# Sixteen groups of three unread products in the attention schedule of a two-layer tower

## The chip, the core and the metric

The kernel runs on one core of a Trainium2 chip. The metric is the device time of one launch in microseconds, the median of several runs. The engines of the core are TensorE (PE, with its weight loads PEld), VectorE (DVE), ScalarE (ACT), GpSimd (POOL) and SyncE (SP), each with an instruction queue of its own; they meet through semaphores. TensorE writes its results to PSUM, eight banks of 128x512 float32, and VectorE or ScalarE copy them out. TensorE's clock is granted at one of two levels, 1.2 and 2.4 GHz, which the profile shows as 0.50 and 1.00.

## What is computed

```
h = tok(x)                              # relu(x W0) * (x W1), then Wo
h = layernorm(h + attention0(h))        # 16 heads of 16, window |i-j| <= 64
h = layernorm(h + quantised_ffn(h))     # int8-like rows, ternary weights, relu(g)^2 * u
h = layernorm(h + attention1(h))        # 16 heads of 16, causal
h = layernorm(h + moe(h))               # 8 experts, top 2, capacity 640, own layernorm inside
```

There are 4 batches of 512 tokens with 256 channels. Nothing of this is changed by the change: its products are written to PSUM and read by nobody.

## The kernel before

The first part of the kernel (up to about 580 us of the profile) is a software pipeline over 256 attention half steps; the second part is the eight experts and the final norms. A unit `u` is one key tile of four heads of one batch in one layer: 128 units, each of two half steps. At half step `n` the pipeline computes the scores of half `n` (L870), the transposed scores of half `n - 15` (L892), and, every second half step, the products of probabilities and values of half `n - 19` (L908). VectorE takes the row maxima from each score bank (L1159), GpSimd splits them in parts (L576 to L582), ScalarE exponentiates the transposed scores (L683), and GpSimd masks them (`affine_select`, L556, L561, L564). Every eighth half step there is a transpose back of four heads (L918) and a division on VectorE (L1174, L1176).

All else, the dense work, is laid between the half steps by the table `DENSE`: a phase, its index and the half step at which it begins; `STEPS` says how many steps it has. `SCHED` lists for each half step what falls on it. The phases that matter here:

- `o`: output projection and layernorm of one batch in one layer (index 0 to 3 for the first layer). Steps 0 and 1 turn the attention output, steps 2 and 3 multiply (L1031), step 4 takes the moments on VectorE (L1183, L1190, L1194) and the root on GpSimd (L587), steps 5 and 6 write the normed rows on ScalarE (L720).
- `ffn`: the quantised layer. Steps 0 and 1 take row maxima on VectorE (L1276), step 2 scales on ScalarE (L808), step 3 rounds on VectorE (L1294), step 6 transposes (L944 on TensorE, copied by ScalarE at L697), and from step 7 on come the gate and up products (L935).
- `gate` and `route`: logits of the experts (L1068, L1074) and the choice of two of them on VectorE (L1215 to L1270), with the counts on TensorE (L1081, L1084).
- `qkv`: transposes of the normed rows (L925, copied at L702) and the projections (L1005, L1014), with the copies L768 and L769.

The first layer's `o` begins at half steps 54, 86, 118 and 150, its `ffn` at 61, 93, 125 and 157; `route` of batches 0 and 1 begins at 188 and 219.

PSUM banks are given out ahead of time: seven banks rotate (the eighth, `V_BANK`, holds the value sums), and `take` gives each product the bank that came free earliest in the plan. Before TensorE writes a bank it waits until that bank's last content was read (`opened`, `d_open`). On TensorE the order in a half step is: scores, then the early dense work (`early`), then row parts (L877), transposed scores, values, back, and last the other dense work (`dense`).

Once, ahead of the experts, the kernel already has 38 unread products (L1592) of the form that the change uses, `mm(bank(0), identb[:, :], qgu[:, 0, 0:S], start=True, stop=True)`.

Of the kernel before, what the change touches and what calls it, by code (L numbers as in the profile page):

```python
# [147 lines left out]
    return () if t is None else (f"gb{t}", f"ub{t}")  # L148


def stretched(phase, i, c):

    return 2 * c if phase == 'wq' and i or phase == 'send' and i == 1 or phase == 'qkv' and 2 <= i else c
# [27 lines left out]
def dense_take(n, phase, i, key, part):  # L181

    take("d", n, (phase, i, key), READ_LATER.get(phase, {}).get(key[0], 0), part)


for _n in HALVES:
    if 0 <= _n < 2 * UNITS:
        for _i, _ in enumerate(score_heads(_n // 2, _n % 2)):
            take("s", _n, (_n // 2, _n % 2, _i), 0, PARTS[0])
    for _phase, _i, _c in SCHED.get(_n, ()):  # L190
        for _key in early_units(_phase, _c):
            dense_take(_n, _phase, _i, _key, PARTS[4])
    if (_n - TO_ROWS) % 8 == 0 and 0 <= _n - TO_ROWS < 2 * UNITS:
        take("t", _n, ("n", (_n - TO_ROWS) // 8), 0, PARTS[1])
    if 0 <= _n - TO_TURNED < 2 * UNITS:
        _u, _h = divmod(_n - TO_TURNED, 2)
        for _i, _ in enumerate(turned_heads(_u, _h)):
            T_LAST[_u] = (_u, _h, _i)
            take("t", _n, (_u, _h, _i), 0, PARTS[2])
    if (_n - TO_BACK) % 8 == 0 and 0 <= _n - TO_BACK < 2 * UNITS:  # L200
        take("s", _n, ("b", (_n - TO_BACK) // 8), TO_HEADS - TO_BACK, PARTS[3])
    for _phase, _i, _c in SCHED.get(_n, ()):
        for _key in dense_units(_phase, _c):
            dense_take(_n, _phase, _i, _key, PARTS[5])
# [11 lines left out]
def build(nc, xT, w01, wtok, wattn, wo, battn, bvcol, brow, wq0, wdn, wgate, consts, masks, w1, w2, b1, b2, lnrow, out):  # L216
# [3 lines left out]
    with ctx:  # L220
# [122 lines left out]
        with ExitStack() as c2:  # L343
# [498 lines left out]
            def _(pe):  # L842
# [38 lines left out]
                def scores_T(u, half):  # L881
# [6 lines left out]
                    for i, heads in enumerate(turned_heads(u, half)):  # L888
# [4 lines left out]
                                     qs[0:KM, r, hd, lo:hi], start=True, stop=True)  # L893
                        ins.then_inc(t_full((u, half, i))[0], 1)

                def values(u):
                    g, kt = divmod(u, NT)
                    s = u // (NG * NT)
                    lo, hi = q_range(kind_of(u), kt)
                    pe.wait_ge(sel_done, u + 1)  # L900
                    if kt == 0:
                        pe.wait_ge(*d_out(("qkv", s, "v1")))
                    if kt == 0 and g:
                        pe.wait_ge(ot_done, g)
                    p = probs_of(u)
                    for j in range(HG):
                        hd = g % NG * HG + j
                        ins = mm(bank(V_BANK)[32 * j:32 * j + 32, lo:hi],  # L908
                                 vaug[:, s % NV, kt, hd * SLOT:hd * SLOT + 32], p[:, j, :],
                                 start=(kt == 0), stop=(kt == NT - 1), skip_group_check=True,  # L910
                                 tile_position=(0, 32 * j))
                    ins.then_inc(pv_mm, 1)
# [24 lines left out]
                        ins.then_inc(d_full(key)[0], 1)  # L937

                def early(phase, i, c):
                    if phase == "ffn" and c == FQT:  # L940
                        pe.wait_ge(fq_done, i + 1)
                        o = d_open(("ffn", i, "fqT")).bitcast(BF16)
                        for n in range(2 * NT):
                            ins = pe.transpose(o[:, n * P:(n + 1) * P], fqb[:, n * P:(n + 1) * P],  # L944
                                               identb[:, :])
                        ins.then_inc(d_full(("ffn", i, "fqT"))[0], 1)
                    if phase == "ffn" and tile_at(c, 1) is not None:
                        quantised_half(i, tile_at(c, 1), 1)
# [885 lines left out]
```

## Time and profile before

| | before |
|---|---|
| median of 3 runs | 926.13 us (925.48 to 926.74) |
| the profiled execution | 926.73 us |
| its span, first to last instruction | 924.6 us |
| TensorE busy | 834.7 us, 90% |
| VectorE, ScalarE, GpSimd busy | 495.4, 433.1, 376.6 us |
| mean granted TensorE clock | 0.951 |

The profiled execution has 2.1 us around its span and lies 0.6 us above the median. Busy time of TensorE has modelled ends, so it tells where TensorE had anything in flight, not that it worked at its peak. The page also cuts the span in 40 slices with the busy tenths of each engine and the granted clock; the trace gives the same for any stretch.

### The profile page before, as it was taken

How to read it: one execution, taken by the hardware profiler on the slowest of the kernel's cores; microseconds unless marked ns; L12 is line 12 of the kernel's file. 1: busy time of each engine (PE TensorE's matmuls, PEld its weight loads, DVE VectorE, ACT ScalarE, POOL GpSimd, SP SyncE). 2: the span in 40 equal slices, each digit the busy share in tenths (PEclk: the TensorE clock that was granted, in tenths of full speed). 3: DMA queues.
4: the chain of work that ended last, by engine and by line, in shares of the span. 5: the costliest groups of instructions: out<-in, count | busy, mean ns of one | idle time of the engine just before them, and what ended most of it. 6: DMA issues, size and time to landing. Idle time of an engine off the chain costs nothing.

```text
span 924.6 us, 14104 instructions
## 1 busy us (share of the span) xinstructions
PE 834.7 (90%) x4796; PEld 536.8 (58%) x4796; DVE 495.4 (54%) x1899; ACT 433.1 (47%) x792; POOL 376.6 (41%) x549
## 2 busy tenths in 40 slices
PE   6999999899899899899999997699999999999920
PEld 2665546556556455355545454277787787787820
DVE  5675344779788798788768764231131230220246
ACT  1525335688787787888566664132202202112005
POOL 6336224656465373253483635701231221220423
PEclk9999999999899899999899999799999999999975
DMA  9662021212202220210332206420423523512342
GB/s 344 218 232 75 25 70 30 60 53 70 71 7 65 70 55 18 70 47 25 110 99 64 72 31 234 144 75 9 145 50 111 149 27 128 153 19 62 40 108 91
DMA packets 58662, 81.47 MB, mean 88 GB/s; under 512 B 8160, under 2 KB 52193, under 8 KB 56160
## 3 DMA queue, kind: packets, MB, share of 16 engines
q1 hardware_dynamic: 49232, 70.22, 23.6%
q0 software_dynamic: 7296, 9.47, 6.0%
q10 hardware_dynamic: 2064, 0.90, 0.4%
q8 instruction: 38, 0.62, 0.3%
q14 instruction: 32, 0.26, 0.1%
HBM read 35.37 MB, written 19.68 MB: 60 GB/s over the span
## 4 chain that ended last, share of the span: by engine, by line
PE 76%; DVE 11%; issue 4%; ACT 4%; POOL 3%; DMA 1%; SPq 0%; POOLq 0%; ACTq 0%; DVEq 0%
PE ps L1572 15%; PE ps L1586 15%; PE ps L959 6%; PE ps L908 6%; PE ps L1005 5%; PE ps L870 5%; PE ps L892 4%; DVE junk L1159 4%; PE ps L1031 3%; PE ps L976 3%; PE ps L1014 3%; PE ps L925 2%; PE ps L935 2%; ACT probs L683 1%; PE ps L1041 1%
## 5 line engine op out<-in xcount | busy, mean ns | idle before, releaser
L1159 DVE CUSTOM_DVE_ANT_0 junk<-ps,maskb 128x256 bf16<-128x256 f32 (+4 forms) x512 | 200.2, 435 | 82.6 <-PE ps L870 82.1
L683 ACT ACTIVATE probs<-ps 128x512 f32<-128x512 f32 (+1 forms) x304 | 156.9, 551 | 61.0 <-PE ps L892 58.9
L1613 ACT ACTIVATE hTe<-ps,qs 128x640 f32<-128x640 f32 x64 | 50.8, 794 | 218.8 <-PE ps L1572 218.8
L1520 POOL DMA_INDIRECT mixed_rows<-ysb,ids x40 | 62.1, 1553 | 221.4 <-DVE ysb L1688 218.4
L1586 PE MATMUL ps<-ks,hTe 128*128 128x256 f32 x640 | 143.3, 379 | 0.0
L1572 PE MATMUL ps<-dxT,qs 128*128 128x320 f32 x512 | 140.1, 433 | 1.2 <-DVE dxT L1666 1.2
L1586 PEld LDWEIGHTS ps<-ks,hTe 128*128 128x128 f32 x640 | 119.3, 190 | 15.1
L1572 PEld LDWEIGHTS ps<-dxT,qs 128*128 128x128 f32 x512 | 96.7, 190 | 40.5 <-DVE dxT L1666 0.9
L870 PE MATMUL ps<-ks,qs 96*128 96x256 bf16 (+4 forms) x512 | 106.5, 291 | 3.8 <-DVE nmax L1159 2.0
L892 PE MATMUL ps<-qs,ks 99*128 99x256 bf16 (+4 forms) x512 | 103.6, 288 | 6.5 <-DVE nmax L1159 3.5
L908 PE MATMUL ps<-probs,vaug 128*32 128x256 f32 (+4 forms) x1024 | 89.3, 422 | 6.5 <-ACT oT L692 3.3
L870 PEld LDWEIGHTS ps<-ks,qs 96*128 96x128 bf16 x512 | 44.4, 101 | 82.5 <-issue 64.8
L1666 DVE COPY dxT<-ps 128x256 f32<-128x256 f32 x40 | 16.6, 420 | 128.6 <-PE ps L1550 128.6
L561 POOL TENSOR_SCALAR_AFFINE_SELECT probs<-probs 128x256 f32<-128x256 f32 (+1 forms) x64 | 38.4, 600 | 96.1 <-ACT probs L683 95.9
L1685 DVE TENSOR_TENSOR ysb<-ps,ks 128x256 f32<-128x256 f32 x40 | 17.0, 425 | 110.2 <-PE ps L1586 110.2
L556 POOL TENSOR_SCALAR_AFFINE_SELECT probs<-probs 128x512 f32<-128x512 f32 x64 | 41.3, 648 | 66.7 <-ACT probs L683 66.4
L959 PE MATMUL ps<-x_sb,tokw 128*128 128x512 f32 x128 | 61.7, 615 | 7.5 <-DMA tokw<-w 7.5
L892 PEld LDWEIGHTS ps<-qs,ks 99*128 99x128 bf16 x512 | 44.5, 101 | 30.9 <-issue 7.3
L1005 PE MATMUL ps<-actT,aw 128*128 128x512 f32 x128 | 60.5, 598 | 1.9 <-issue 1.1
L1159 DVE DVE_READ_ACCUMULATOR2_ANT nmax<- 128x1 f32 x512 | 42.2, 82 | 0.0
L908 PEld LDWEIGHTS ps<-probs,vaug 128*32 128x32 f32 x1024 | 20.7, 110 | 37.0 <-issue 25.3
L959 PEld LDWEIGHTS ps<-x_sb,tokw 128*128 128x128 f32 x128 | 23.2, 195 | 31.2 <-issue 31.0
(199 smaller groups left out, 1244.3 us busy)
## 6 DMA issues: line engine op xcount, KB each, us to landing
qs<-parts SPq DMA_DIRECT2D x96, 128.0 KB, 2.4
ks<-parts SPq DMA_DIRECT2D x96, 128.0 KB, 2.4
qs<-w SPq DMA_DIRECT2D x8, 1024.0 KB, 9.6
ks<-w SPq DMA_DIRECT2D x8, 1024.0 KB, 4.9
dispatched_rows<-att SPq DMA_DIRECT2D x8, 650.0 KB, 10.9
ks<-dispatched_rows SPq DMA_DIRECT2D x4, 650.0 KB, 7.4
x_sb<-xT SPq DMA_DIRECT2D x8, 256.0 KB, 4.0
mixed_rows<-h SPq DMA_DIRECT2D x4, 512.0 KB, 3.1
```

The lines of the kernel that those rows point to most:

```text
L556: pool.affine_select(out=p[:, :, 0:P], in_=p[:, :, 0:P], compare_op=ALU.is_ge, fill=0.0, base=0, pattern=[[0, HG], [1, P]], channel_multip ...
L683: act.activation(probs_of(u)[:, heads[0]:heads[-1] + 1, :], turned_bank((u, half, i))[:, 0:len(heads) * w].rearrange("p (j n) -> p j n", n=w),
L870: ins = mm(o[:, a * (hi - lo):(a + 1) * (hi - lo)], qs[0:KS, r, hd, t * P:(t + 1) * P], ks[0:KS, r, hd, lo:hi], start=True, stop=True)
L892: ins = mm(o[:, a * (hi - lo):(a + 1) * (hi - lo)], ks[0:KM, r, hd, kt * P:(kt + 1) * P], qs[0:KM, r, hd, lo:hi], start=True, stop=True)
L908: ins = mm(bank(V_BANK)[32 * j:32 * j + 32, lo:hi], vaug[:, s % NV, kt, hd * SLOT:hd * SLOT + 32], p[:, j, :], start=(kt == 0), stop=(kt = ...
L959: ins = mm(o, tokw[:, k, col:col + P], x_sb[:, k, :], start=(k == 0), stop=(k == KD - 1))
L1005: ins = mm(o, w[:, k, col:col + P], actT[:, k, :], start=(k == 0), stop=(k == KD - 1))
L1159: ins = dve.tensor_tensor_reduce(out=junk[:, b - (b > V_BANK), a * (hi - lo):(a + 1) * (hi - lo)], in0=score_bank((u, half, i))[:, a * (hi ...
L1520: pool.indirect_dma_start(out=acc, out_offset=bass.IndirectOffsetOnAxis(ap=ids[:, e, t:t + 1], axis=0), in_=ysb[:, e % 2, t, :], in_offset ...
L1572: ins = mm(bank(2 * (n % 2) + c)[:, 0:HC], w1s[:, e % 2, k, m * P:(m + 1) * P], dxT[:, e % 2, k, c * HC:(c + 1) * HC], start=(k == 0), sto ...
L1586: ins = mm(bank(4 + n % 2)[:, 0:D], hTe[:, e % 2, m, t * P:(t + 1) * P], w2s[:, e % 2, m, :], start=(m == 0), stop=(m == MH - 1))
L1613: act.activation(hTe[:, e % 2, m, :].rearrange("p (a n) -> p a n", a=2), ps[:, 2 * (n % 2):2 * (n % 2) + 2, 0:HC], ACT.Silu, bias=b1s[:, e ...
```

## The change

Three unread products, 128x512 in bfloat16 each, are put at certain half steps as early work, right behind the scores of that half step and ahead of the transposed scores. They take a bank of the rotation, wait until its former content was read, write it three times, and count it as filled and as read themselves. The condition `filled_up` holds for steps 4 and 6 of `o` of the first layer's four batches (half steps 58 and 60, 90 and 92, 122 and 124, 154 and 156), for step 0 of the four `ffn` (61, 93, 125, 157), and for steps 2 and 3 of `route` of batches 0 and 1 (190, 191, 221, 222): 16 half steps and 48 products. The plan of banks is made anew with these takes in it; 82 of the other takes have another use before them than they had, all of them within eight half steps behind a group.

```
+UNREAD = 3
+
+def filled_up(phase, i, c):
+    return (phase == "o" and i < B and c in (4, 6) or phase == "ffn" and c == 0
+            or phase == "route" and i < 2 and c in (2, 3))
...
     for _phase, _i, _c in SCHED.get(_n, ()):
+        if filled_up(_phase, _i, _c):
+            dense_take(_n, _phase, _i, f"x{_c}", PARTS[4])
         for _key in early_units(_phase, _c):
...
+                def unread(key, count):
+                    o = d_open(key)
+                    for n in range(count):
+                        ins = mm(o, identb[:, :], qgu[:, 0, 0:S], start=True, stop=True)
+                        if n == 0:
+                            ins.then_inc(d_full(key)[0], 1)
+                    ins.then_inc(d_out(key)[0], 1)
...
                 def early(phase, i, c):
+                    if filled_up(phase, i, c):
+                        if phase == "o" and i == 0 and c == 4:
+                            pe.wait_ge(w_taken, 2)
+                        unread((phase, i, f"x{c}"), UNREAD)
```

On TensorE, at half steps 58 to 61, the program before reads as follows (L870 scores, L892 transposed scores, L908 values, L918 back):

```order
L870 MATMUL ps<-ks,qs 128x256 x2
L892 MATMUL ps<-qs,ks 128x256 x2
L870 MATMUL ps<-ks,qs 128x256 x2
L877 MATMUL ps<-identb,nparts 48x128
L892 MATMUL ps<-qs,ks 128x256 x2
L908 MATMUL ps<-probs,vaug 32x192 x4
L870 MATMUL ps<-ks,qs 128x256 x2
L892 MATMUL ps<-qs,ks 128x256 x2
L918 MATMUL ps<-cst,oT 128x128 x4
L870 MATMUL ps<-ks,qs 128x256 x2
L892 MATMUL ps<-qs,ks 128x192 x2
```

And after the change, with the same work under new line numbers (L881 scores, L903 transposed scores, L928 values, L938 back, L911 the unread products):

```order
L881 MATMUL ps<-ks,qs 128x256 x2
L911 MATMUL ps<-qgu,identb 128x512 x3
L903 MATMUL ps<-qs,ks 128x256 x2
L881 MATMUL ps<-ks,qs 128x256 x2
L888 MATMUL ps<-identb,nparts 48x128
L903 MATMUL ps<-qs,ks 128x256 x2
L928 MATMUL ps<-probs,vaug 32x192 x4
L881 MATMUL ps<-ks,qs 128x256 x2
L911 MATMUL ps<-qgu,identb 128x512 x3
L903 MATMUL ps<-qs,ks 128x256 x2
L938 MATMUL ps<-cst,oT 128x128 x4
L881 MATMUL ps<-ks,qs 128x256 x2
```

Nothing else moved: a group of three now stands between the scores and the transposed scores at half steps 58 and 60, and a third one follows the last row shown, at 61. The second place is the routing of batch 0 on TensorE, at half steps 190 to 192; after the change it reads:

```order
L881 MATMUL ps<-ks,qs 128x512 x2
L911 MATMUL ps<-qgu,identb 128x512 x3
L881 MATMUL ps<-ks,qs 128x512 x2
L911 MATMUL ps<-qgu,identb 128x512 x3
L903 MATMUL ps<-qs,ks 128x512 x2
L928 MATMUL ps<-probs,vaug 32x256 x4
```

and before:

```order
L870 MATMUL ps<-ks,qs 128x512 x4
L892 MATMUL ps<-qs,ks 128x512 x2
L908 MATMUL ps<-probs,vaug 32x256 x4
L870 MATMUL ps<-ks,qs 128x128 x2
L892 MATMUL ps<-qs,ks 128x512 x2
```

Here the second pair of scores has three unread products ahead of it and the transposed scores have six.

## Rows read from the trace of the kernel before

**Rows 1.** The page: span, and TensorE's granted clock in 40 slices, in tenths.
```profile
span 924.6 us, 14104 instructions
...
PEclk9999999999899899999899999799999999999975
```
**Rows 2.** Busy time by stretch: us from:to, length, PE PEld DVE ACT POOL, clock, DMA.
```profile
178.30:181.70 3.40, 1.88 (x20) 0.84 (x18) 3.37 (x17) 1.97 (x5) 1.57 (x3) 0.99 0.02 5
181.70:188.50 6.80, 5.92 (x37) 3.73 (x37) 5.03 (x26) 6.32 (x14) 4.68 (x12) 0.50 0.60 162
...
243.10:249.90 6.80, 5.94 (x37) 3.82 (x38) 4.97 (x26) 6.23 (x14) 4.68 (x12) 0.50 0.75 203
...
304.60:311.40 6.80, 6.06 (x39) 3.86 (x40) 4.57 (x26) 6.24 (x14) 4.89 (x12) 0.50 0.74 203
...
376.20:379.60 3.40, 3.33 (x18) 2.69 (x18) 1.72 (x10) 3.40 (x9) 1.64 (x3) 0.50 0.56 153
...
441.10:447.90 6.80, 6.80 (x30) 3.47 (x31) 5.30 (x24) 2.33 (x5) 1.77 (x4) 0.50 0.20 54
...
505.90:512.70 6.80, 6.69 (x32) 2.01 (x32) 4.48 (x28) 4.10 (x9) 2.07 (x6) 0.50 0.60 179
```
**Rows 3.** Timeline of PE from half step 61 on: start, us, what, idle before.
```profile
178.03 0.38 PE L870 MATMUL ps<-ks,qs 96*128 96x256 bf16 x2
179.09 0.34 PE L892 MATMUL ps<-qs,ks 99*128 99x192 bf16 x2 [0.68 <-DVE nmax L1159]
...
181.45 0.33 PE L892 MATMUL ps<-qs,ks 99*128 99x192 bf16 x2 [0.84 <-ACT probs L683]
182.66 1.08 PE L908 MATMUL ps<-probs,vaug 128*32 128x256 f32 x8 [0.88 <-POOL probs L564]
...
186.80 1.87 PE L925 MATMUL ps<-cst,h 128*128 128x128 f32 x8
...
191.11 1.03 PE L935 MATMUL ps<-qgu,work 128*128 128x512 bf16 x4
```
**Rows 4.** Busy time by stretch, columns as in Rows 2.
```profile
182.20:190.70 8.50, 8.04 (x62) 5.18 (x63) 5.37 (x27) 7.59 (x17) 4.61 (x11) 0.63 0.63 170
...
373.70:381.30 7.60, 6.54 (x45) 3.81 (x45) 4.35 (x22) 7.16 (x16) 2.62 (x6) 0.78 0.44 120
364.70:371.50 6.80, 6.46 (x46) 2.62 (x44) 6.52 (x29) 4.21 (x11) 2.49 (x4) 1.00 0.14 36
...
446.20:451.00 4.80, 4.22 (x31) 1.51 (x27) 4.52 (x22) 2.27 (x6) 0.87 (x5) 0.82 0.74 200
498.80:506.40 7.60, 6.00 (x45) 2.34 (x43) 7.19 (x28) 4.10 (x10) 1.73 (x4) 0.97 0.50 135
...
178.00:182.70 4.70, 2.29 (x26) 1.01 (x27) 4.50 (x24) 2.97 (x7) 2.47 (x4) 0.89 0.18 45
...
221.40:224.90 3.50, 2.17 (x24) 1.01 (x22) 3.36 (x10) 3.44 (x7) 2.49 (x5) 1.00 0.50 141
```
**Rows 5.** Timeline of POOL and ACT around the same place.
```profile
177.32 0.64 POOL L564 TENSOR_SCALAR_AFFINE_SELECT probs<-probs 128x512 f32<-128x512 f32 x1
...
178.37 1.04 POOL L587 TENSOR_TENSOR rstd<-mv,neg_half 128x4 f32<-128x4 f32 x1 [0.41 <-DVE mv L1194]
...
189.71 1.00 ACT L697 ACTIVATE work<-ps 128x1024 bf16<-128x1024 bf16 x1
```
**Rows 6.** The chain that ended last, in time, at 176 to 196: start, us, what.
```profile
178.37 1.05 POOL rstd L587
...
182.66 1.08 PE ps L908 x8
...
187.00 1.66 PE ps L925 x8
```
**Rows 7.** Timeline of DVE and ACT at 371 us and in the routing, where they meet PE.
```profile
371.33 0.68 DVE L1159 CUSTOM_DVE_ANT_0 junk<-ps,maskb 128x512 bf16<-128x512 f32 x1
...
448.38 1.09 ACT L683 ACTIVATE probs<-ps 128x512 f32<-128x512 f32 x2 [2.84 <-PE ps L892]
...
451.13 0.87 ACT L683 ACTIVATE probs<-ps 128x384 f32<-128x384 f32 x2 [0.47 <-PE ps L892]
...
512.74 0.56 DVE L1159 CUSTOM_DVE_ANT_0 junk<-ps,maskb 128x384 bf16<-128x384 f32 x1 [2.15 <-PE ps L870]
```

## The prediction

> **What bounds the kernel now.** I read the clock row of the page first. TensorE is granted full speed nearly everywhere, with an 8 in slices 11, 14, 17 and 23 and a 7 in slice 26 [rows 1]. Then I cut the places of the dips out as stretches [rows 2]. There are six ahead of 520 us: 1.2 GHz for 6.8 us from 181.7, from 243.1, from 304.6, from 441.1 and from 505.9, and for 3.4 us from 376.2. The first four belong to `o` and the start of `ffn` of batches 0 to 3, the last two to `route` of batches 0 and 1. That is where the change puts its products, so its effect must be read there.
>
> What comes before such a fall is to be seen at the first one, which the second and third repeat nearly to the tenth. From 178.3 to 181.7 TensorE was busy 1.88 of 3.40 us and VectorE 3.37 [rows 2]. TensorE waits three times, 0.68 us for row maxima, 0.84 us for ScalarE, 0.88 us for GpSimd's mask [rows 3]. So ahead of the fall the chain runs over VectorE, the root on GpSimd at 178.37, and ScalarE [rows 6], and TensorE has 4.70 - 2.29 = 2.41 us to spare between 178.0 and 182.7 [rows 4]. From 182.66 on the chain lies on TensorE [rows 6], now at half clock. So the spare time is where products cost little, and the stretch behind it is where the clock is worth something.
>
> **What the change adds.** Per group three products of the form of L935, of which four take 1.03 us with the end of the last modelled at 0.38 us: (1.03 - 0.38) / 3 = 0.217 us each [rows 3]. A group is 0.65 us at full clock and twice that, 1.3 us, at half. 48 of them are 10.4 us of TensorE. The waits for banks cost nothing where I followed them: the bank of a group was last used two half steps earlier or more, and VectorE or ScalarE has read it by then. The one wait for the quantised weights is long fulfilled.
>
> **Batches 0 to 2 (three times the same).** The three groups are 1.95 us against 2.41 us of spare time, so they nearly fit. One thing leaks: the group at half step 58 stands ahead of the transposed scores, so ScalarE's exponentials and GpSimd's masks of that step come 0.65 us later. The second mask ends at 177.32 + 0.64 = 177.96 and the root starts at 178.37 [rows 5], so 0.41 us of the 0.65 are covered and the root, on the chain, is late by 0.24 us. The rest of the groups pushes scores and values into what was idle; VectorE has its scores in time.
>
> Does the clock then stay? The spare time in 178.0 to 182.7 sinks from 2.41 to some 0.7 us (2.41 - 1.95 + 0.24), a busy share of 85%. The trace has a stretch without a fall that is much thinner than that: 221.4 to 224.9, TensorE busy 2.17 of 3.50 us, 62%, clock 1.00 [rows 4]. Nearest to it on the other side is 178.3 to 181.7 with 55%. So I take the clock as kept.
>
> What a kept clock brings is not half of 6.8 us. On the chain TensorE has 188.5 - 182.66 = 5.8 us at half clock, so the upper bound is 2.9 us. But ScalarE is next: from 182.2 to 190.7, where its copy L697 of the first quantised transposes ends (189.71 + 1.00 [rows 5]), it is busy 7.59 of 8.50 us [rows 4]. It can only lose its 0.91 us of idle time. TensorE's gate product L935 needs that copy and starts today at 191.11 [rows 3], 0.40 us after it, because TensorE itself was late; at full clock that goes too. 0.91 + 0.40 = 1.3 us, less the 0.24 of the late root: 1.0 us gained per batch, with 0 and 2.9 us as bounds. I take the value of the ScalarE row, since it is measured at the place. Three times: **-3.0 us**. From 191 on TensorE bounds, and keeps the gain.
>
> **Batch 3.** Here the causal units begin and TensorE has hardly any room: 6.80 - 6.46 = 0.34 us from 364.7 to 371.5 [rows 4]. 1.95 - 0.34 = 1.6 us of products push the scores back. VectorE, which carries the chain there, takes the maxima of half step 158 at 371.33 [rows 7], about 0.9 us after TensorE had them, so it is late by 0.6 to 0.7 us. The late scores close the later gap, so the fall at 376.2 should go as well. It covers 3.4 us, so at most 1.7 us come back; ScalarE has only 0.44 us of idle time from 373.7 to 381.3 [rows 4], with a wait like the one at L935 behind it. I take 1.0 us back and 0.6 us lost: **-0.4 us** (bounds +1.6 and -1.7).
>
> **Routing of batch 0.** The fall at 441.1 comes before the groups of half steps 190 and 191, which lie at 446.2 and later; nothing of the change is ahead of it, so it stays. The first group runs at half clock, 1.3 us, the second at full, 0.65 us, together 1.9 us, against 0.58 us of TensorE's idle time from 446.2 to 451.0 [rows 4]. So the transposed scores come some 1.3 us later. ScalarE waits for them today (2.84 us), and has 0.47 us to spare before its next wait [rows 7]; VectorE, on the chain, has its scores early enough. Bounds 0 and +1.9 us; I take **+0.5 us**, near ScalarE's slack.
>
> **Routing of batch 1.** VectorE is busy 7.19 of 7.60 us from 498.8 to 506.4, TensorE idle 1.6 us [rows 4], so two groups (1.3 us) are hidden. They are over by 503.3, and TensorE stays thin after that, up to the fall at 505.9. I take this fall as staying: **0**. If it went, the stretch after it is TensorE's alone, with VectorE waiting 2.15 us at its end [rows 7]: -2.5 us.
>
> **Sum.** -3.0 - 0.4 + 0.5 + 0 = -2.9 us. Against the profiled execution, 926.73 us (span 924.6), that is 923.8 us; that execution lies 0.6 us above the median, so against 926.13 us it is **923.2 us**.
>
> **A rule that speaks against it.** TensorE ran from 186.80 to 188.67 nothing but the transposes of L925 [rows 3], and the clock rose at 188.5 [rows 2]. The Trainium skill, TensorE: Matmul & The Clock Gate, Part 4: PE-mode transpose, says that the full clock doesn't engage for transposes, because they don't count as busy in the same way. The trace does not agree, since the clock rose at the end of just such a stretch. What the rule's result would be here: the fall is only put off to the transposes that stand in each of the four batches, nothing comes back, and 3 x 0.24 + 0.6 + 0.5 = +1.8 us are lost. I give that 0.03 and count it with rival 2.
>
> **Rivals.**
> 1. *The fall in the routing of batch 1 goes too.* For it: the groups end 2.6 us ahead of it. Against: TensorE stays thin to the last. -2.9 - 2.5 = -5.4: 920.7 us.
> 2. *Slower: falls are moved into TensorE's own stretches.* If the clock is lost some 3.4 us later, at about 185, again for 6.8 us, it stays low until 191.9, where TensorE is the chain. The 3.4 us from 188.5 to 191.9 then run at half speed, 1.7 us more, while 185 to 188.5 is half clock in both. At full clock from 181.7 to 185 TensorE wins at most 1.2 us, since ScalarE bounds. So +0.5, with the late root +0.7 per batch: +2.1, for batch 3 +0.6, routing +0.5: +3.2 us, 929.3 us. It decides from the moment that the clock is not granted at 185. Against it: the 85% above.
> 3. *The gain is taken back.* All that follows moves against the moments at which the clock is decided. The stretch at 221.4 and one like it at 283 are thin; a fall in one puts 6.8 us of half clock where TensorE bounds for much of it, some 2 to 3 us. -2.9 + 2.5 = -0.4: 925.7 us. Or the falls stay and the products are hidden but for the late roots and the routing: +0.7 + 0.5 = +1.2: 927.3 us. Between them 926.5 us.
>
> **Chances.** Forecast 0.48, rival 1 0.14, rival 2 0.14, rival 3 0.24. A measurement tells about 0.2%, 1.9 us, from no change. Forecast and rival 1 are faster by more, but for some 0.06 of the forecast where the gain per batch is nearer 0.6 us: faster 0.56. Rival 3 and that: same 0.30. Rival 2: slower 0.14. The range reaches from rival 1 with a little more from ScalarE's side (920.0) to short of rival 2 (927.8).
>
> **What would show it.** Right: the stretches after half steps 58, 90 and 122 at clock 1.00, ScalarE without idle time up to L697, the interval from one `o` to the next shorter by 1.0 us, the fall by the logits of batch 0 still there. Batch 3: the maxima of half step 158 0.6 us later against the work before. Wrong: a clock of 0.50 within 8 us behind any first-layer group, or a new one near 221 or 283 us; GpSimd's root later by more than 0.24 us; or TensorE late at half step 62, which would say that the groups did not fit in the waits.

## The result, and the profile after

| | before | changed |
|---|---|---|
| median beside each other on one chip | 925.95 us (925.48 to 926.74, 4 runs) | 919.64 us (919.21 to 921.91, 4 runs) |
| ratio, 95% interval | | 0.9934 (0.9919 to 0.9949) |
| profiled execution, span | 926.73, 924.6 us | 921.91, 919.8 us |
| mean granted TensorE clock | 0.951 | 0.963 |

The changed kernel is faster by 6.3 us. Forecast were 2.9 us: the sign was right, the time lies below the low end of the range (920.0). Run again on two chips ("all, again" and "all, third" below) it stood at 0.9937 (0.9920 to 0.9953) and 0.9943 (0.9921 to 0.9964), by the medians 5.9 and 5.8 us. The profiled execution of the changed kernel is the slowest of its four. On the chip of the first four experiments two of the 26 runs of before took 1,592 and 1,707 us; they are left out of its median below.

The page of the changed kernel: span, busy time (14,178 instructions are 74 more than before: 48 weight loads and 25 of the 48 products, of which some have no record in the trace) and the clock row.

```profile
span 919.8 us, 14178 instructions
...
PE 833.0 (91%) x4821; PEld 535.8 (58%) x4844; DVE 497.2 (54%) x1899; ACT 430.7 (47%) x792; POOL 376.2 (41%) x549
...
PEclk9999999999999999999899998799999999999975
```

Ahead of 620 us the row of before [rows 1] has an 8 in slices 11, 14 and 20 and a 7 in slice 26. Now 11 and 14 show a 9, 20 still an 8 and 26 a 7, and slice 25 has a new 8: the fall at 567.4 us of before stands at 552.1, and the long one behind it begins at 572.6. There are 48 products more, and yet TensorE is busy 1.7 us less.

The places of the falls, cut out as in [rows 2] and [rows 4]: us from:to, length, PE PEld DVE ACT POOL, clock, DMA.

```profile
176.90:180.30 3.40, 3.40 (x28) 1.83 (x27) 3.33 (x18) 1.35 (x3) 1.94 (x3) 1.00 0.04 8
183.10:190.60 7.50, 6.10 (x65) 3.87 (x65) 6.04 (x33) 7.46 (x17) 4.90 (x12) 1.00 0.67 182
224.40:227.90 3.50, 3.26 (x16) 2.59 (x17) 2.69 (x14) 2.54 (x5) 0.56 (x1) 0.51 0.02 4
285.90:289.30 3.40, 3.40 (x18) 2.60 (x17) 2.78 (x13) 2.24 (x3) 0.39 (x2) 0.50 0.02 4
372.80:376.20 3.40, 2.30 (x18) 0.69 (x16) 3.01 (x15) 3.05 (x7) 1.34 (x4) 1.00 0.74 200
439.50:446.30 6.80, 6.58 (x30) 3.41 (x31) 5.51 (x24) 2.23 (x5) 1.76 (x4) 0.50 0.23 61
504.80:511.40 6.60, 6.38 (x55) 2.90 (x55) 6.36 (x37) 4.71 (x11) 3.29 (x8) 1.00 0.67 198
```

The falls behind the groups of batches 0 to 3 are gone, and so is the one in the routing of batch 1. The one in the routing of batch 0 stays. Two new ones of 3.4 us have come, at 224.4 and 285.9.

A half step is one turn of the pipeline, and a stage is here the time from one half step to another. To see what each fall is worth I read the start of the scores (L870 before, L881 after) of certain half steps from the timeline of PE, in every profiled execution, and took the differences. A stage is named by its half steps. For the first stage the two starts are, before, 168.30 and 195.60, and here in the changed kernel:

```profile
169.17 0.34 PE L881 MATMUL ps<-ks,qs 96*128 96x192 bf16 x2
...
195.14 0.34 PE L881 MATMUL ps<-ks,qs 96*128 96x192 bf16 x2
```

27.3 us became 26.0. All stages, in us ("all, again" and "all, third" are the changed kernel run again; the others are the experiments below; the last column is the span). Left out are 134 to 150 (36.2 or 36.3 everywhere), 167 to 186 (46.2 everywhere), 199 to 217 (32.4 to 32.9) and 232 to 255 (30.0 or 30.4).

| profiled execution | 54-70 | 70-86 | 86-102 | 102-118 | 118-134 | 150-167 | 186-199 | 217-232 | span |
|---|---|---|---|---|---|---|---|---|---|
| before | 27.3 | 32.3 | 29.1 | 32.3 | 29.5 | 34.6 | 24.2 | 24.3 | 924.6 |
| changed | 26.0 | 33.9 | 27.2 | 34.0 | 27.8 | 33.8 | 24.6 | 21.7 | 919.8 |
| all, again | 26.0 | 32.3 | 27.7 | 34.0 | 27.8 | 33.8 | 24.6 | 21.7 | 917.3 |
| all, third | 26.0 | 32.3 | 27.7 | 34.0 | 27.8 | 33.8 | 23.9 | 21.5 | 918.6 |
| first layer | 26.0 | 32.3 | 27.7 | 33.9 | 27.8 | 33.8 | 24.5 | 21.7 | 921.2 |
| routing only | 26.1 | 32.3 | 27.9 | 32.3 | 29.5 | 34.6 | 24.6 | 21.7 | 922.9 |
| eight columns | 27.4 | 32.3 | 29.1 | 32.3 | 29.6 | 34.7 | 24.1 | 21.7 | 921.9 |
| no routing 0 | 26.0 | 33.9 | 27.3 | 34.0 | 27.8 | 33.8 | 24.1 | 21.7 | 920.1 |
| guarded | 26.0 | 32.3 | 27.6 | 32.3 | 28.2 | 33.8 | 26.1 | 21.7 | 919.1 |
| no batch 3 | 26.0 | 32.3 | 27.7 | 34.0 | 27.8 | 34.3 | 23.8 | 21.7 | 916.2 |
| one group | 25.6 | 32.3 | 27.3 | 32.3 | 27.9 | 33.3 | 23.8 | 21.7 | 914.1 |
| one group, again | 25.6 | 32.3 | 27.3 | 32.3 | 27.9 | 34.3 | 26.3 | 21.7 | 921.6 |
| one group, routing 0 | 25.6 | 32.3 | 27.3 | 32.3 | 27.9 | 33.3 | 23.8 | 24.3 | 917.6 |
| one group, routing 1 | 25.6 | 32.3 | 27.3 | 32.3 | 27.9 | 33.3 | 26.2 | 21.7 | 918.1 |
| one group alone | 25.6 | 32.3 | 27.3 | 32.3 | 27.9 | 34.3 | 26.1 | 21.7 | 921.5 |
| early group | 26.4 | 32.3 | 28.2 | 33.9 | 28.2 | 34.3 | 26.2 | 24.6 | 927.8 |
| one product | 26.1 | 33.9 | 27.4 | 34.0 | 27.4 | 34.4 | 26.5 | 24.6 | 926.6 |
| late start | 27.7 | 32.3 | 29.2 | 32.3 | 29.6 | 34.7 | 24.1 | 21.7 | 930.0 |

The sum for "all, again" against before, up to the scores of half step 255 (541.0 against 546.8), in unrounded starts: -0.4 at the start, -1.3 and -1.4 and -1.8 for batches 0 to 2, +1.7 for the new fall at 284, -0.8 for batch 3, +0.4 and -2.7 for the two routings, and +0.4 for 232 to 255: -5.8 us. The last +0.4 belongs to the routing of batch 1: that stage takes 30.0 us in the four profiles with its fall and 30.4 in the fourteen without, so the missing fall is worth 2.3 us, not 2.7. Behind half step 255, where nothing was changed, "all, again" takes 376.3 us against 377.8, another -1.5; but "all, third", the same kernel, takes 378.1 there.

The first three falls can be counted over all eighteen profiles. In the twelve with a group of three full products at step 0 of `ffn` none of the three is there. In the six without it ("before", "routing only", "eight columns", "early group", "one product", "late start") the first and second are always there, with 3.4 or 6.8 us, and the third is missing in "one product" alone.

### The profile page after: what moved, and what is told of

It reads as the page before. It is cut to its first block, busy times and chain, and to the rows that moved or that the text cites. A ratio compares the mean times of both kernels' runs of the same rounds, so it can differ in the third digit from the quotient of the medians.

```text
span 919.8 us, 14178 instructions
## 1 busy us (share of the span) xinstructions
PE 833.0 (91%) x4821; PEld 535.8 (58%) x4844; DVE 497.2 (54%) x1899; ACT 430.7 (47%) x792; POOL 376.2 (41%) x549
## 4 chain that ended last, share of the span: by engine, by line
PE 74%; DVE 8%; ACT 5%; issue 5%; POOL 4%; DMA 3%; SPq 0%; POOLq 0%; ACTq 0%; DVEq 0%
PE ps L1596 15%; PE ps L1610 15%; PE ps L983 6%; PE ps L928 5%; PE ps L1029 5%; PE ps L881 5%; PE ps L903 4%; PE ps L1000 3%; PE ps L1055 3%; PE ps L1038 3%; DVE junk L1183 3%; PE ps L955 2%; ACT probs L694 2%; POOL dispatched_rows L632 2%; PE ps L1065 2%
## 5 line engine op out<-in xcount | busy, mean ns | idle before, releaser
L1637 ACT ACTIVATE hTe<-ps,qs 128x640 f32<-128x640 f32 x64 | 50.8, 794 | 218.4 <-PE ps L1596 218.4
L881 PE MATMUL ps<-ks,qs 96*128 96x256 bf16 (+4 forms) x512 | 104.1, 285 | 2.5 <-DVE nmax L1183 1.3
L903 PE MATMUL ps<-qs,ks 99*128 99x256 bf16 (+4 forms) x512 | 101.2, 284 | 1.4 <-DVE nmax L1183 0.9
L928 PE MATMUL ps<-probs,vaug 128*32 128x256 f32 (+4 forms) x1024 | 86.6, 410 | 6.4 <-ACT oT L703 3.2
L881 PEld LDWEIGHTS ps<-ks,qs 96*128 96x128 bf16 x512 | 43.2, 99 | 79.0 <-issue 61.4
L1029 PE MATMUL ps<-actT,aw 128*128 128x512 f32 x128 | 60.5, 598 | 1.9 <-issue 1.1
L903 PEld LDWEIGHTS ps<-qs,ks 99*128 99x128 bf16 x512 | 43.9, 99 | 25.6 <-issue 3.1
L928 PEld LDWEIGHTS ps<-probs,vaug 128*32 128x32 f32 x1024 | 20.4, 108 | 36.6 <-issue 23.6
```

Source lines behind the costliest of these rows:

```text
L881: ins = mm(o[:, a * (hi - lo):(a + 1) * (hi - lo)], qs[0:KS, r, hd, t * P:(t + 1) * P], ks[0:KS, r, hd, lo:hi], start=True, stop=True)
L903: ins = mm(o[:, a * (hi - lo):(a + 1) * (hi - lo)], ks[0:KM, r, hd, kt * P:(kt + 1) * P], qs[0:KM, r, hd, lo:hi], start=True, stop=True)
L928: ins = mm(bank(V_BANK)[32 * j:32 * j + 32, lo:hi], vaug[:, s % NV, kt, hd * SLOT:hd * SLOT + 32], p[:, j, :], start=(kt == 0), stop=(kt = ...
L1029: ins = mm(o, w[:, k, col:col + P], actT[:, k, :], start=(k == 0), stop=(k == KD - 1))
L1637: act.activation(hTe[:, e % 2, m, :].rearrange("p (a n) -> p a n", a=2), ps[:, 2 * (n % 2):2 * (n % 2) + 2, 0:HC], ACT.Silu, bias=b1s[:, e ...
```

## The experiments

**First layer alone** (the groups of `route` left out) and **routing alone** (those of `o` and `ffn` left out). Here and below, where the group of step 4 of `o` of batch 0 is left out and others stay, the one wait for the quantised weights moves to the first group that is left; "early group" keeps it.

```
 def filled_up(phase, i, c):
-    return (phase == "o" and i < B and c in (4, 6) or phase == "ffn" and c == 0
-            or phase == "route" and i < 2 and c in (2, 3))
+    return phase == "o" and i < B and c in (4, 6) or phase == "ffn" and c == 0
```
```
+    return phase == "route" and i < 2 and c in (2, 3)
```

> Only the twelve groups of the first layer's o and ffn; the four of the routing are left out. Theory A (each group works where it stands: a kept clock brings 1.4 us per batch 0 to 2, 0.8 us for batch 3, and the two groups of routing 1 alone keep the clock there): the fall near 500 to 510 us comes back, the time is 2.0 to 2.5 us above the changed kernel, about 921.8 us. Rival B (the fall in routing 1 went only because everything before it had moved by some us): no fall there either, and about 919.2 us.

> Only the four groups of the two routings; the twelve of the first layer are left out, so all falls up to 441 us stay where they were. Theory A: the fall at 505.9 is gone, -2.5 us there, +0.4 us for routing 0: about 923.9 us. Rival B: the fall at 505.9 stays, about 926.4 us.

Measured: the first layer alone 923.98 us, ratio 0.9975 (0.9960 to 0.9990); routing alone 927.49 us, 1.0005 (0.9993 to 1.0016), where before took 926.96 us on that chip. The table shows the first layer's gain without the routing's groups: 26.0, 27.7, 27.8 and 33.8. The two medians together give 2.4 us less than before, not the 6: in single executions more than the edit differs. In "first layer" the fall in the routing of batch 1 is missing although no group is there (21.7), and the time behind half step 255 is 379.5 us, 1.4 to 3.2 us more than in the three profiles of the changed kernel; in "routing only" the falls at 183 and 244 last 3.4 us, not 6.8, although nothing stands ahead of them that before doesn't have, and stages 54 to 70 and 86 to 102 are 1.2 us shorter (26.1, 27.9). So a profile of one execution can't price a group, and a stage is only as good as the number of executions that agree.

**Eight columns.** Each product is cut to 8 of its 512 columns; banks, waits and places are as in the changed kernel. It asks whether the gain is the clock's or that of the new plan of banks.

```
-                        ins = mm(o, identb[:, :], qgu[:, 0, 0:S], start=True, stop=True)
+                        ins = mm(o[:, 0:8], identb[:, :], qgu[:, 0, 0:8], start=True, stop=True)
```

> All sixteen groups, the same plan of banks and the same waits, but each unread product has 8 columns instead of 512, so there is next to no work in them. Theory A (the gain is the clock's): all six falls stay, time 926 us, within 0.5 us. Rival C (the gain comes from the other plan of banks): 920 to 922 us.

Measured: 925.13 us, 0.9987 (0.9975 to 1.0000). The falls of batches 0 to 2 are where they were, 6.8 us each, and the stages are before's to 0.1 us: 27.4, 29.1, 29.6, 34.7. The line of the products in the groups of this kernel, and under it the stretch of the first fall:

```profile
L911 PE MATMUL ps<-qgu,identb 128*128 128x8 bf16 x48 | 3.6, 169 | 0.7 <-DVE att L1200 0.7
```
```profile
182.10:188.90 6.80, 6.10 (x38) 3.92 (x39) 4.78 (x24) 6.08 (x14) 4.68 (x12) 0.50 0.74 200
```

So in the first layer the gain is the clock's: it needs the columns, not the banks. In the routing of batch 1 this kernel has no fall either (21.7), which is taken up below.

**No routing 0** (the groups of batch 0's routing left out) and **no batch 3** (those of `o` and `ffn` of batch 3 left out).

```
-            or phase == "route" and i < 2 and c in (2, 3))
+            or phase == "route" and i == 1 and c in (2, 3))
```
```
-    return (phase == "o" and i < B and c in (4, 6) or phase == "ffn" and c == 0
+    return (phase == "o" and i < 3 and c in (4, 6) or phase == "ffn" and i < 3 and c == 0
```

> The changed kernel without the two groups of routing 0 (half steps 190 and 191). Theory A: they lie behind a fall that has already happened and cost 0.4 us, so 919.2 us. Rival D: they help the clock to rise sooner or keep it later, so 920 us or more.

> Without the three groups of batch 3 (half steps 154, 156, 157). Theory A2: the fall near 376 us is back and the groups' cost of 0.6 us gone; half steps 150 to 167 took 34.6 us before and 33.8 with the groups, so the time is 0.8 us above the changed kernel. Rival: the fall at that place hangs on the moment only, and leaving the groups out changes nothing or gains 0.6 us.

Measured: 922.44 us, 0.9961 (0.9944 to 0.9979) without routing 0, the chip of the first three; 919.88 us, 0.9935 (0.9918 to 0.9952) without batch 3, beside 920.15 for the changed kernel on its chip. In the stages: with the groups in routing 0 it takes 24.6 us, without them 24.1, since the fall stays at 439.7; that is the 0.5 us of the forecast. Batch 3 takes 33.8 us with its groups, 34.6 in before and 34.3 here, where the fall (372.2) is still 3.4 us long. So they bring 0.5 to 0.8 us in the stage, which the medians can't confirm: without them the kernel is 0.3 us faster, within the noise.

**Guarded** (no groups in routing 0, and one more group at step 22 of `ffn` of batches 0 and 1, half steps 83 and 115, ahead of the new falls).

```
-    return (phase == "o" and i < B and c in (4, 6) or phase == "ffn" and c == 0
-            or phase == "route" and i < 2 and c in (2, 3))
+    return (phase == "o" and i < B and c in (4, 6) or phase == "ffn" and (c == 0 or i < 2 and c == 22)
+            or phase == "route" and i == 1 and c in (2, 3))
```

> The changed kernel once more, as the yardstick for the others of this call and for a second look at its falls. Theory A2 (what the first four runs left: the groups of the first layer keep the clock where they stand; the thin stretches near 221, 283 and 506 us and in 548 to 553 fall or not by where they lie against the moments at which the clock is decided): the stretches from half step 54 to 70 and from 118 to 134 take 25.9 and 27.8 us again, those near 221 and 283 may fall or not, and with it the time moves by 1.6 us each. Rival: the falls at 221 and 283 are there every time.

> Without the two groups of routing 0, and with one more group at half steps 83 and 115 (step 22 of ffn of batches 0 and 1), where TensorE waits 0.75 and 0.78 us for ScalarE. Theory A2: no fall near 221 and 283, half steps 70 to 86 and 102 to 118 take 32.3 us as before the change instead of 33.9; with routing 0 at -0.5 us that is 1 to 3.5 us below the changed kernel of this call, the more the oftener those falls come. Rival: the added 1.3 us of products are on the chain, and the time is the same or longer.

Measured: guarded 920.24 us, 0.9930 (0.9911 to 0.9949); the changed kernel again 920.15 us, 0.9937. In the guarded kernel both thin stretches are at full clock, 32.3 and 32.3 us. The changed kernel has a fall at 283.5 in this profile too, but none at 224. The same stretches, "all, again" and then "guarded":

```profile
219.00:227.00 8.00, 6.46 (x74) 4.24 (x73) 7.72 (x32) 7.23 (x14) 4.24 (x7) 1.00 0.31 84
283.50:286.90 3.40, 3.40 (x17) 2.67 (x18) 2.64 (x13) 2.33 (x4) 0.29 (x2) 0.50 0.02 4
```
```profile
219.00:227.00 8.00, 7.11 (x65) 4.18 (x64) 7.72 (x31) 7.55 (x14) 4.81 (x7) 1.00 0.44 119
```

At 219 the extra group takes TensorE from 6.46 to 7.11 us busy and moves neither VectorE (7.72) nor the stage. That the guards kept the falls away isn't shown by this one profile: "all, again" has none at 221 without a guard, and "one group" below none at 283. What was saved at 283 was lost elsewhere: the routing of batch 0 took 26.1 us, because its fall came later (446.7) and hit TensorE's own stretch.

**One group.** Only the group at step 0 of each first-layer `ffn`, the last of the three, right ahead of the thin stretch; with the routing's groups (twice, on two chips), alone, and with one routing each.

```
-    return (phase == "o" and i < B and c in (4, 6) or phase == "ffn" and c == 0
+    return (phase == "ffn" and c == 0
             or phase == "route" and i < 2 and c in (2, 3))
```

> Of the three groups per batch in the first layer only the one at step 0 of ffn (half steps 61, 93, 125, 157); the routing groups as in the change. Theory E (what counts is that the stretch just ahead of the fall holds products; the earlier groups only make GpSimd's root 0.3 us late): the clock is kept, half steps 54 to 70 take 25.6 us, and the time is about 1 us below the changed kernel. Theory F (all three are needed, since they push TensorE's own work into the gap): the falls are back, 27.3 us for 54 to 70, and the time is 3 to 5 us above the changed kernel.

> Only the one group per batch at step 0 of ffn (half steps 61, 93, 125, 157), no groups in the routing: 12 products in all. Theory A2 (the routing groups buy nothing that lasts; the stretch 217 to 232 takes 21.7 us without them too): the same as with the routing groups, 915.5 to 917.5 us. Rival: the groups of routing 0 or 1 do keep the clock in the routings, and without them 2 to 3 us are lost: 918 to 919 us.

> The one-group kernel with both routings' groups once more, on the chip of this call. Theory K (the groups of routing 0 keep the clock whenever the fall would come late, at 445 us and after, and cost 0.5 us when it comes early): 915.5 to 918 us, half steps 186 to 199 in 23.8 or 24.6 us, never 26.1. Rival L (916 us was that chip's luck): 920 to 923 us, as the kernel without routing groups took on another chip.

> One group per batch in the first layer and the groups of routing 0 only. Theory K: half steps 186 to 199 in 23.8 or 24.6 us; the time within 1 us of the kernel with both routings' groups. Rival L: 26.1 us for 186 to 199, 920 to 923 us.

> One group per batch in the first layer and the groups of routing 1 only. Theory K: half steps 186 to 199 in 24.1 or 26.1 us, and the time 1 to 4 us above the kernel with both routings' groups. Rival L: no difference between the two.

> The changed kernel, for the same chip. Theory K: 919 to 921 us, 186 to 199 in 24.6 or 23.8 us; 2 to 5 us above the one-group kernel, of which 0.9 to 1.2 us from GpSimd's root in four batches and the rest from falls near 221 and 283 us that the one-group kernel misses. Rival L: the two within 1 us.

| | us | ratio to before, 95% |
|---|---|---|
| one group | 915.92 | 0.9901 (0.9876 to 0.9925) |
| all, again (same chip) | 920.15 | 0.9937 (0.9920 to 0.9953) |
| one group alone | 921.98 | 0.9948 (0.9928 to 0.9968) |
| one group, again | 923.26 | 0.9947 (0.9927 to 0.9966) |
| one group, routing 0 | 920.88 | 0.9938 (0.9914 to 0.9961) |
| one group, routing 1 | 921.29 | 0.9938 (0.9917 to 0.9960) |
| all, third (same chip as the last three) | 921.66 | 0.9943 (0.9921 to 0.9964) |

In all five the first three falls are gone with a third of the products, the first stage takes 25.6 us (26.0 with three groups), and no new fall comes at 224 or 283. The 0.4 us (25.6 in place of 26.0) go with the root, since here nothing stands ahead of the transposed scores of half step 58. It starts 10.1 us behind half step 54, as before; in the changed kernel 10.4 us. "One group", then the changed kernel, timeline of POOL:

```profile
178.48 1.04 POOL L598 TENSOR_TENSOR rstd<-mv,neg_half 128x4 f32<-128x4 f32 x1 [0.41 <-DVE mv L1218]
```
```profile
179.58 1.04 POOL L598 TENSOR_TENSOR rstd<-mv,neg_half 128x4 f32<-128x4 f32 x1
```

The group itself lies in a wait, which the timeline of PE of "one group" shows, and the values behind it follow after a wait for GpSimd's mask as before:

```profile
179.50 0.59 PE L911 MATMUL ps<-qgu,identb 128*128 128x512 bf16 x2 [0.99 <-DVE nmax L1183]
...
182.76 0.64 PE L928 MATMUL ps<-probs,vaug 128*32 128x256 f32 x8 [0.79 <-POOL probs L575]
```

But its total isn't settled: the same kernel took 915.9 us on one chip and 923.3 on another, 4.2 us under the changed kernel there and 1.6 us over it here. Five of the six runs on the first chip took 915.5 to 916.5 us and one 921.8; the seven on the other took 920.6 to 923.7. The two profiles differ mainly in three places: 150 to 167 (33.3 and 34.3), 186 to 199 (23.8 and 26.3), and the time behind half step 255 (376.2 and 379.8). In each the second has a fall that the first hasn't. Behind 255 that explains a part only: from the first to the last product of the experts the fall at 595 makes 286.1 us of 284.9, 1.2 us more, but 2.5 us lie ahead of it, up to the first of these products (50.8 and 53.3), where both have a fall of 13.7 us. "One group", then the three of "one group, again":

```profile
PEclk9999999999999999999999999799999999999975
```
```profile
370.00:373.40 3.40, 3.38 (x19) 1.99 (x20) 2.41 (x14) 3.40 (x9) 1.98 (x5) 0.50 0.54 144
445.10:451.90 6.80, 6.80 (x38) 2.33 (x38) 4.46 (x25) 3.45 (x8) 1.90 (x6) 0.50 0.44 135
595.30:598.70 3.40, 2.88 (x9) 1.60 (x8) 0.91 (x3) 0.00 (x0) 3.40 (x6) 0.50 0.13 44
```

The fall in routing 0 was absent in "one group", "no batch 3" and "one group, routing 0", early (437 to 442) or short in most others, and late (444 to 450) in six (that of "late start", at 445.3, counts as early by its own start); late the stage takes 26.1 to 26.5 us, against 24.1 or 24.2 for an early one of 6.8 us (24.6 with the groups in place) and 23.8 for none. With two full groups there it came late in 1 of 8 profiled executions, without them in 5 of 10. Theory K of the expectations is out: with the groups of routing 0 the fall still came late once (26.3 us), and the kernel without them ("routing 1") took 2.0 us less than that one, not 1 to 4 more. In routing 1 the count is clearer: with groups no fall in 10 of 10, without them (or with eight columns) a fall in 4 of 8: before, "one group, routing 0", "early group" and "one product". The nearest pair is "one group, routing 0" and "one group", alike in every stage before, 24.3 and 21.7 us. The fall in the former:

```profile
498.70:505.50 6.80, 6.75 (x32) 2.04 (x33) 4.52 (x28) 4.14 (x9) 2.06 (x6) 0.50 0.61 180
```

**Early group and one product.** Does a smaller edit keep the clock? Tried are the group at step 4 of `o` alone, or the `ffn` group with one product of 512 columns and one of 8; neither has groups in the routings.

```
-    return (phase == "o" and i < B and c in (4, 6) or phase == "ffn" and c == 0
-            or phase == "route" and i < 2 and c in (2, 3))
+    return phase == "o" and i < B and c == 4
```
```
-UNREAD = 3
+UNREAD = 2
...
+    return phase == "ffn" and c == 0
...
-                        ins = mm(o, identb[:, :], qgu[:, 0, 0:S], start=True, stop=True)
+                        cols = 8 if n else S
+                        ins = mm(o[:, 0:cols], identb[:, :], qgu[:, 0, 0:cols], start=True, stop=True)
```

> Only the group at step 4 of o (half steps 58, 90, 122, 154), some 2.5 us earlier than the group of the one-group kernel, no others. Theory E (the products must stand in the thin stretch just ahead of the fall): the falls stay, half steps 54 to 70 take 27.3 us or, with GpSimd's root late, 27.6, and the time is 925 to 927 us. Rival G (any extra products in the neighbourhood do): 54 to 70 in 25.9 us and 919 us or less.

> The one group at step 0 of ffn, but with one product of 512 columns and one of 8 in place of three of 512. Theory H (a single product is too little): the falls of the four batches are back in most runs, 923 to 926 us. Theory I (a third of the work is enough): no falls there, 915.5 to 917.5 us as with three.

Measured: 928.30 us, 1.0013 (0.9998 to 1.0029), and 928.28 us, 1.0017 (0.9995 to 1.0038); before 926.72 on that chip. Both still fall at 183.9, for 3.4 us instead of 6.8:

```profile
183.90:187.30 3.40, 3.22 (x24) 1.44 (x24) 2.76 (x14) 3.36 (x9) 1.96 (x7) 0.50 0.75 204
```
```profile
183.90:187.30 3.40, 3.40 (x28) 1.68 (x21) 2.75 (x15) 3.35 (x9) 2.20 (x7) 0.50 0.64 174
```

The first is "early group", the second "one product". The stage is shorter than before (26.4 and 26.1 us), but both get a fall at 286, a late one in the routing of batch 0 and one in that of batch 1 ("one product" also one at 225, while the one at 305 is missing), and their medians lie 1.6 us above before's, which the intervals can't tell from no change. So three products at step 0 keep the clock; one there (with one of 8 columns) doesn't in two of three batches, and three at half step 58 don't in any. That these made the fall shorter isn't shown, since "routing only" has 3.4 us there too, with no group near.

**Late start.** The kernel before, with one small load ahead of everything that SyncE waits for.

```
+                sp.dma_start(x_sb[:, 0, 0:128], xT[0, 0:P, 0:128]).then_inc(late, 16)
+                sp.wait_ge(late, 16)
```

> The kernel before with one small load that SyncE waits for ahead of all others, which puts everything about 2 us later and changes nothing else. Theory J (where a thin stretch lies against the moments at which the clock is decided sets how long a fall lasts, and whether the one at 506 us comes): other lengths of the falls than before (3.4 in place of 6.8 us at one of the first three, or none near 506), and so a time that is not 2 us longer but 1 us shorter to 1 us longer. Rival: the same six falls, 2 us longer.

Measured: 930.96 us, 1.0043 (1.0030 to 1.0057), 4.2 us later than before. The load cost more than the 2 us expected: the start of half step 54 moved from 168.3 to 171.8, and the falls of batches 0 to 2 moved with it, at their old length. But the fall in the routing of batch 1 is not there (505.8 to 512.6 is at 1.00), and there is one at 602.3 instead:

```profile
185.90:192.70 6.80, 6.57 (x41) 4.33 (x42) 4.49 (x23) 6.08 (x13) 4.37 (x11) 0.50 0.75 204
...
505.80:512.60 6.80, 5.14 (x41) 2.06 (x41) 6.55 (x33) 4.20 (x10) 2.27 (x8) 1.00 0.74 203
```

A shift of the start alone thus takes the fall at 505.9 away, as the prediction's third rival has it of falls in general; it doesn't take the first three.

## Why the prediction was wrong

Two terms failed. The fall in the routing of batch 1 was taken as staying, at 0, and is missing in all three profiles of the changed kernel, 2.3 us; what of that the groups bring stays open. And the gain per batch of the first layer, 1.0 us, was too small by 0.3 to 0.8, since ScalarE could lose more than its idle time. New falls of 1.6 to 1.7 us took part of that back.

**What bounds the kernel, and where.** Right. All that the change did up to half step 255, it did at the falls of the clock. One reading is wrong: the row has its 8s in slices 11, 14 and 20, not 11, 14, 17 and 23 [rows 1]. Nothing hangs on it, because the six falls were read from the stretches.

**Batches 0 to 2: right mechanism, term too small.** The clock is kept, from the groups to the first quantised transposes and on, also through the transposes (L945, at 186.28): 183.1 to 190.6 is at 1.00 in the rows above, and no fall follows before 224. Rival 2, which had its fall at 185, is out. By the Trainium skill, TensorE: Matmul & The Clock Gate, Part 4: PE-mode transpose, the full clock doesn't engage for transposes; this trace doesn't agree. The gain was put at 1.0 us per batch; in the profiles it is 1.3 to 1.8 (27.3 to 26.0, 29.1 to 27.2 or 27.7, 29.5 to 27.8, taken unrounded). The term that was too small comes from "it can only lose its 0.91 us of idle time". ScalarE's copy of the quantised transposes ended at 190.71 before [rows 5]. In the changed kernel (its half step 54 starts 0.87 us later) it is the last of these rows of the timeline of ACT:

```profile
187.49 0.58 ACT L703 ACTIVATE oT<-ps 128x512 f32<-128x512 f32 x1
187.97 0.59 ACT L694 ACTIVATE probs<-ps 128x512 f32<-128x512 f32 x1
...
189.56 1.02 ACT L708 ACTIVATE work<-ps 128x1024 bf16<-128x1024 bf16 x1
```

It ends at 190.58, or 189.71 with the 0.87 taken off: 1.00 us earlier, and that after a root that is late. Before, the same two read so:

```profile
186.29 0.58 ACT L692 ACTIVATE oT<-ps 128x512 f32<-128x512 f32 x1
187.04 0.60 ACT L683 ACTIVATE probs<-ps 128x512 f32<-128x512 f32 x1 [0.17 <-PE ps L892]
```

From one start to the next are 0.75 us before and 0.48 us after, 0.27 us less, where the idle time between them is 0.17. An instruction that follows without a wait starts before the one ahead shows its end, so its whole 0.58 us isn't paid; one that waits pays it. By my estimate from this pair (0.27 - 0.17) each wait that goes brings some 0.1 us beyond its idle time. That would be 0.4 us for the four waits that ScalarE has in 187.04 to 189.54 before: 0.91 + 0.4 - 0.34 = 1.0 us, as measured at this copy; with TensorE's lag of 0.40 it is 1.4. The root was late by 0.34 us instead of 0.24, and the next dense product of TensorE (L1029, 191.97 before, 191.51 - 0.87 = 190.64 after) came 1.33 us earlier. So the three batches bring some 4.5 us in "all, again", not 3.0.

**The falls near 221 and 283.** The prediction named the stretches as thin and gave a fall there to a rival at 0.24. One comes in the profiles of the changed kernel at 284 or 286, three of three, and at 224 in one. It costs 1.6 to 1.7 us, not the 2 to 3 of the rival, since it lasts 3.4 us, not 6.8. That rival had the mechanism right, but took it for the whole outcome: what it takes back is 1.7 us of 4.5 in "all, again" and 3.2 of 4.9 in the first profile. Together the three batches and the new falls make -2.8 us in "all, again" and -1.7 in the first profile. That the one is near the forecast's -3.0 is luck: a gain that was put too small and a fall that was left out.

**Batch 3.** The push was right to the tenth: the scores of half step 158 start 16.3 us behind those of 150 (370.53 - 354.20) in place of 14.7 (369.78 - 355.07), 1.6 us later; VectorE's maxima, put at 0.6 to 0.7 us late, come 0.5 us late (16.76 behind the same start, in place of 16.26). The stage is shorter by 0.8 us, where -0.4 stood. Without the groups ("no batch 3"), the fall as long as before but 0.7 us earlier in the stage, it is 0.3. The two terms can be read apart. With one group and no fall the stage takes 33.3 us; two more groups make it 33.8, 0.5 us, near the 0.6 lost. A fall of 3.4 us makes it 34.3 when it begins 19.9 us behind half step 150 ("one group, again"), 34.4 at 20.7 ("one product") and 34.6 at 21.1 (before): 1.0 to 1.3 us, where 1.0 stood.

**Routing of batch 0.** The +0.5 is what was measured (24.6 against 24.1). ScalarE's wait at the transposed scores grew from 2.84 us [rows 7] to 4.24, 1.4 us, where 1.3 was worked out. What the step left out is that the fall can move: with the groups, a late one costs 1.7 us more (26.3) and none at all saves 0.8 (23.8).

**Routing of batch 1: the step that failed.** "I take this fall as staying" gave 0; measured are -2.7 us in the stage (24.3 to 21.7) and +0.4 in the next, -2.3 together, with -2.5 worked out in the same step, as rival 1 at 0.14. The ground, that TensorE is thin between the groups and the fall, was no ground: in the first layer the clock is kept although TensorE waits 0.79 us for the mask behind the last group. Here the changed kernel has it at 1.00 from 504.8 to 511.4. The groups are not the only thing that does it. Before, run later, has it missing by a late start alone, and "eight columns" and "first layer" by less. The runs show that with groups it came in none of ten profiles and without them in four of eight; what they don't show is how much of the 2.3 us in a median is owed to the groups. "Routing only", whose profile hasn't the fall, is in the median of ten runs no faster than before (1.0005).

**The sum.** -0.4 at the start, -4.5 and +1.7 in the first layer, -0.8, +0.4, -2.3, and -1.5 behind half step 255, together some -7.3 us in "all, again"; the medians say -5.8 to -6.3. Where the forecast (-2.9) missed 3.4 us, 2.3 are the fall in routing 1; rival 1, the forecast with this fall gone, stood at 920.7 us, 1.1 above the result. The last 1.5 us lie in a part that the change doesn't touch. They are no steady gain: "all, third" takes 0.3 us more there than before, and "one group" differs by 3.6 us between its two profiles (376.2 and 379.8).

**What stays open.** What sets the moment at which the clock is decided, so that one kernel has a fall that its twin hasn't; whether "one group" is faster than the changed kernel (the two comparisons contradict each other); and why a fall at 595 comes in some launches.

## What to carry to other kernels

A row of waits of under 1 us on TensorE can cost its clock, and three products that nobody reads, laid in the last of these waits, keep it: 1.3 to 1.8 us for 0.65 us of work that was nearly free. Price such a gain at the engine that comes next, with some 0.1 us for each wait of it that goes; then look where the kernel is thin further on, for the falls that come, go or shift there are worth as much. Run each version several times, since one profile has one draw of these falls.

## What the runs showed of the hardware

- The same products at 8 columns, TensorE waiting at the same places, didn't keep the clock; at 512 columns they did.
- TensorE can be busy and lose the clock. Ahead of the fall at 441.1 of the kernel before it has no idle time at all, but more than half of the stretch is a product of 8 columns with float32 operands, the logits. Ahead of that at 285.9 of the changed kernel it is busy for 1.88 of 3.40 us, as ahead of the first fall of before [rows 2]. The first two rows are of before (windows, and its timeline of PE), the third of the changed kernel:

```profile
437.70:441.10 3.40, 3.40 (x30) 2.28 (x29) 1.74 (x10) 2.18 (x6) 1.58 (x3) 1.00 0.02 4
...
439.61 2.03 PE L1074 MATMUL ps<-gatew,actT 128*128 128x8 f32 x15
```
```profile
282.50:285.90 3.40, 1.88 (x23) 0.97 (x22) 3.20 (x9) 3.35 (x8) 2.46 (x4) 1.00 0.42 116
```

- Most falls lasted 3.4 or 6.8 us, one 10.2. Each of the eighteen profiles also has one of 13.7 or 17.1 us that begins between 567 and 580 us, and one of 38 to 40 us at the end; with the change and without it they are there.
- What a fall costs depends on where it lies. One of 3.4 us cost 1.6 to 1.7 us at 284, 1.0 to 1.3 in batch 3 and 1.2 at 595; one of 6.8 us in the routing of batch 0 0.3 us when early (24.1 for 23.8) and 2.3 to 2.4 when late.
- From one ACTIVATE of 128x512 to the next were 0.48 us where the second didn't wait, though each shows 0.58 to 0.59 us.
- Which falls a launch has depends on when things happen, not only on what: routing alone had 3.4 us instead of 6.8 at 183 and 244 with nothing changed ahead of them, and the same kernel ran at 915.9 and 923.3 us.
